# Gathered chunks of a graph layer rounded and split in pairs, in a ring of six gathered rows and six rounded rows

## The reference

```python
Q = jax.nn.relu(x @ Wq + bq)
V = x @ Wv + bv
# _former: Q = relu(layer_norm(Q)); H from the row sums of Q
out = cosQ @ (cosQ.T @ V) + sinQ @ (sinQ.T @ V)      # divided by a norm per row
# _gcn: deg counts the edges of each dst, dinv = rsqrt(deg)
xw = x @ Wg
gcn = segment_sum(xw[src] * (dinv[src] * dinv[dst])[:, None], dst, N) + bg
y = jax.nn.relu(_layer_norm(out + gcn + V, gamma, beta))
x = _layernorm(x + y, axis=-1)
```

## Time and profile before

| | |
|---|---|
| median of 3 runs | 2114.59 us (2107.7 to 2127.57) |
| the profiled execution | 2113.34 us, span from first to last instruction 2111.5 us |
| granted TensorE clock, mean | 0.908 |
| busy: PE, PEld (weight load) | 1769.9 us (84%), 1402.0 us (66%) |
| busy: DVE, ACT, POOL | 1695.7 (80%), 899.8 (43%), 996.5 us (47%) |
| gathers (L396) | 882, 256 KB each |
| casts (L464), subtractions and one-hots (L769, L766) | 882 of each |

### The profile page before, as it was taken

The page is one execution under the profiler, slowest core; times in us unless marked ns, Lnnn a source line. Parts: engine busy times, 40 slices in busy tenths (PEclk is TensorE's granted clock), DMA queues, the critical chain, the costliest instruction groups (busy, mean ns, idle before and its releaser), DMA issues.

```text
span 2111.5 us, 29877 instructions
## 1 busy us (share of the span) xinstructions
PE 1769.9 (84%) x8579; PEld 1402.0 (66%) x8579; DVE 1695.7 (80%) x3686; ACT 899.8 (43%) x1642; POOL 996.5 (47%) x1056
## 2 busy tenths in 40 slices
PE   3888827999979997979997989988988887997986
PEld 2666625777757774857775867766776676775775
DVE  6888866898868887858776778877887997987997
ACT  1222214556545555535554456655333333332332
POOL 0000006666656666567665657677333443443440
PEclk9999968999989997989998889989888898887897
DMA  3111167877757877667776758767554654654662
GB/s 111 61 51 61 51 226 240 257 249 240 252 177 243 258 231 218 190 197 234 222 231 183 212 182 259 232 217 231 170 165 130 204 180 138 192 173 142 192 192 83
DMA packets 159968, 394.66 MB, mean 187 GB/s; under 512 B 23760, under 2 KB 25420, under 8 KB 159796
## 3 DMA queue, kind: packets, MB, share of 16 engines
q0 software_dynamic: 71120, 233.10, 37.6%
q1 hardware_dynamic: 67544, 121.07, 17.0%
q10 hardware_dynamic: 21132, 38.50, 5.1%
HBM read 341.24 MB, written 51.34 MB: 186 GB/s over the span
## 4 chain that ended last, share of the span: by engine, by line
PE 51%; DVE 30%; issue 9%; ACT 5%; DMA 3%; DVEq 1%; POOL 0%; POOLq 0%; another core or an unknown queue 0%; ACTq 0%; SPq 0%
PE bank L1041 10%; PE bank L1042 10%; PE bank L1040 10%; PE bank L1117 9%; PE bank L1119 7%; DVE stage L716 5%; DVE split L769 3%; DVE bn_parts L964 2%; DVE stage L713 2%; DMA split<-scaled_g,index_slots 2%; DVE rows L769 2%; ACT split L464 2%; PE bank L1070 2%; DVE one_hot L766 2%; DVE operands L726 1%
## 5 line engine op out<-in xcount | busy, mean ns | idle before, releaser
L396 POOL DMA_INDIRECT split<-scaled_g,index_slots x490 | 521.1, 1063 | 395.8 <-PE bank L1119 251.4
L396 POOL DMA_INDIRECT rows<-scaled_g,index_slots x392 | 415.3, 1059 | 210.8 <-PE bank L1119 96.8
L464 ACT CAST split<-split 128x512 fp32r<-128x512 f32 x490 | 299.6, 617 | 427.4 <-PE bank L1119 267.4
L1117 PE MATMUL bank<-split,one_hot 128*128 128x512 f32 x882 | 390.4, 443 | 104.4 <-DVE combine L799 38.2
L769 DVE TENSOR_TENSOR split<-split 128x512 fp32r<-128x512 f32 x490 | 339.4, 693 | 66.0 <-ACT split L464 55.2
L464 ACT CAST split<-rows 128x512 fp32r<-128x512 f32 x392 | 240.4, 618 | 284.0 <-PE bank L1119 222.6
L1040 PE MATMUL bank<-weights,operands 128*128 128x512 f32 x784 | 334.4, 427 | 1.4 <-DVE operands L813 1.4
L1041 PE MATMUL bank<-weights,operands 128*128 128x512 f32 x784 | 322.0, 411 | 0.0
L1042 PE MATMUL bank<-weights,operands 128*128 128x512 f32 x784 | 320.0, 408 | 0.0
L766 DVE TENSOR_SCALAR one_hot<-tile_id,dst_cols 128x128 fp32r<-128x128 f32 x882 | 257.5, 292 | 69.0 <-PE bank L1119 47.2
L1117 PEld LDWEIGHTS bank<-split,one_hot 128*128 128x128 f32 x882 | 172.7, 196 | 183.8 <-DVE rows L769 59.0
(11 more groups left out here) (194 smaller groups left out, 2941.9 us busy)
## 6 DMA issues: line engine op xcount, KB each, us to landing
stage<-in_x SPq DMA_DIRECT2D x144, 256.0 KB, 2.8
stage<-values SPq DMA_DIRECT2D x98, 256.0 KB
scaled_g<-nodes SPq DMA_DIRECT2D x49, 256.0 KB, 3.1
own_rows<-scaled_g SPq DMA_DIRECT2D x49, 256.0 KB
values<-stage ACTq DMA_DIRECT2D x49, 256.0 KB
combine<-values SPq DMA_DIRECT2D x49, 256.0 KB
gcn_plus_values<-combine ACTq DMA_DIRECT2D x49, 256.0 KB
stage<-gcn_plus_values SPq DMA_DIRECT2D x49, 256.0 KB
```

The lines of the kernel that those rows point to most:

```text
L396: pool.indirect_dma_start(out=plain(row_ring[k % RING]), out_offset=None, in_=table, in_offset=bass.IndirectOffsetOnAxis(ap=index_slots[:, ...
L464: act.copy(hi_ring[k % SPLIT], plain(row_ring[k % RING])).then_inc(s["chunk_rounded"], 1)
L1117: pe.matmul(gcn_bank[:, :], one_hot[:, slot, :], hi_ring[slot], start=k == 0, stop=False, skip_group_check=True)
```

## The change

Rows and rounded rows are kept in three pairs each. `split[:, 0:6]` holds the rounded rows, `split[:, 6:8]` and the four rows of `rows` the gathered ones. ACT and DVE act at even k only: ACT waits for both landings of the pair and for `chunk_summed` with `freed(n + 1, 6)` (with n even, the sum of chunk n-5), and rounds 1024 columns at once. DVE makes both one-hots behind one wait (six slots of one-hots now) and subtracts 1024 columns at once. `chunk_rounded` and `chunk_split` count pairs. POOL still gathers each row by itself, into six slots. PE's instructions and their order are the same; it waits for the split at even k only. The extra chunk uses slot 0 as before.

```diff
--- before.py
+++ after.py
@@ -44,8 +44,9 @@
     GROUPS = -(-CHUNKS // P)
     HIST = -(-CHUNKS // TILES)
     PER_TILE = 18
-    RING = 9
-    SPLIT = 3
+    RING = 6
+    SPLIT = 6
+    PAIRS = 3
     BATCH = 6
     COLS = GROUPS * P
     LN_EPS = 1e-5
@@ -153,7 +154,9 @@
                 for n in range(3)]
         g_hi, g_lo = split[:, 0:4, :], split[:, 4:8, :]
         hi_ring = [split[:, n, :] for n in range(SPLIT)]
-        row_ring = [split[:, SPLIT + n, :] if n < 5 else rows[:, n - 5, :] for n in range(RING)]
+        hi_pairs = [split[:, 2 * n:2 * n + 2, :] for n in range(PAIRS)]
+        row_pairs = [split[:, 6:8, :], rows[:, 0:2, :], rows[:, 2:4, :]]
+        row_ring = [row_pairs[n // 2][:, n % 2, :] for n in range(RING)]
 
         def plain(ap):
             return ap.bitcast(F32)
@@ -387,7 +390,7 @@
                 for k in range(PER_TILE):
                     if k % BATCH == 0:
 
-                        wait_apart(pool, s["chunk_rounded"], freed(chunk_number(seq, k + BATCH - 1), PER_TILE))
+                        wait_apart(pool, s["chunk_rounded"], freed(chunk_number(seq, k + BATCH - 1) // 2, PER_TILE // 2))
                         pool.tensor_copy(index_slots[:, k:k + BATCH], src_cols[:, bass.ds(first + k, BATCH)])\
                             .then_inc(s["chunk_indexed"], 1)
                         pool.wait_ge(s["chunk_indexed"], done(seq * (PER_TILE // BATCH) + k // BATCH))
@@ -458,10 +461,12 @@
 
 
             def chunk(seq, k):
-                n = chunk_number(seq, k)
-                act.wait_ge(landed[k % RING], seq * (16 * PER_TILE // RING) + 16 * (k // RING + 1))
-                act.wait_ge(s["chunk_summed"], freed(n, SPLIT))
-                act.copy(hi_ring[k % SPLIT], plain(row_ring[k % RING])).then_inc(s["chunk_rounded"], 1)
+                if k % 2 == 0:
+                    n, pair = chunk_number(seq, k), k // 2 % PAIRS
+                    for r in (k % RING, k % RING + 1):
+                        act.wait_ge(landed[r], seq * (16 * PER_TILE // RING) + 16 * (k // RING + 1))
+                    act.wait_ge(s["chunk_summed"], freed(n + 1, SPLIT))
+                    act.copy(hi_pairs[pair], plain(row_pairs[pair])).then_inc(s["chunk_rounded"], 1)
 
             def extra_chunks(seq):
                 first = act.value_load(column(schedule, seq), min_val=0, max_val=CHUNKS - 1)
@@ -760,13 +765,16 @@
                 return first
 
             def chunk(seq, k, first):
-                n = chunk_number(seq, k)
-
-                dve.wait_ge(s["chunk_summed"], freed(n, SPLIT))
-                dve.tensor_scalar(one_hot[:, k % SPLIT, :], tile_id[:, :], column(dst_cols, first + k), None,
-                                  ALU.is_equal).then_inc(s["chunk_hot"], 1)
-                dve.wait_ge(s["chunk_rounded"], done(n))
-                dve.tensor_tensor(row_ring[k % RING], plain(row_ring[k % RING]), plain(hi_ring[k % SPLIT]), ALU.subtract)\
+                if k % 2:
+                    return
+                n, pair = chunk_number(seq, k), k // 2 % PAIRS
+
+                dve.wait_ge(s["chunk_summed"], freed(n + 1, SPLIT))
+                for c in (k, k + 1):
+                    dve.tensor_scalar(one_hot[:, c % SPLIT, :], tile_id[:, :], column(dst_cols, first + c), None,
+                                      ALU.is_equal).then_inc(s["chunk_hot"], 1)
+                dve.wait_ge(s["chunk_rounded"], done(n // 2))
+                dve.tensor_tensor(row_pairs[pair], plain(row_pairs[pair]), plain(hi_pairs[pair]), ALU.subtract)\
                     .then_inc(s["chunk_split"], 1)
 
             def add_own(seq):
@@ -1113,7 +1121,8 @@
                 if k == 0:
 
                     pe.wait_ge(s["gcn_combined"], freed(seq, 1))
-                pe.wait_ge(s["chunk_split"], done(chunk_number(seq, k)))
+                if k % 2 == 0:
+                    pe.wait_ge(s["chunk_split"], done(chunk_number(seq, k) // 2))
                 pe.matmul(gcn_bank[:, :], one_hot[:, slot, :], hi_ring[slot], start=k == 0, stop=False,
                           skip_group_check=True)
                 pe.matmul(gcn_bank[:, :], one_hot[:, slot, :], row_ring[k % RING], start=False, stop=False,
```

## The result

The changed kernel takes 2271.59 us (median of four runs, 2258.16 to 2276.42), beside 2115.98 us for the kernel before in the same comparison: a ratio of 1.072, 95% interval 1.065 to 1.079. It is slower by 7.2%, where 2174 us was forecast, and the time lies 17 us above the range (2105 to 2255). The profiled execution has a span of 2267.2 us, 155.7 more than before.

A forecast was written before the change was run, and what follows sets the result against it. PE was taken to bound the Q/V, cosine and sine stages, DVE and PE both full in the output stage. Pauses +60, output stage -6 and refills +7 made +61 on 2113 us: 2174 us, range 2105 to 2255.

The forecast's parts named there:

- a loop of 7.2 us: From the sum that frees a slot to the pair's first matmul on PE: 7.2 us, between 6.35 and 8.1.
- a landing of 4.1 us: Gather start to cast start: 4.1 us, the middle of 3.24 (drained kernel) and 4.96 (full flow).
- two or three equal pauses a tile: PE pauses once per ring turn: 2 a tile in Q/V and sine, 3 in cosine; 60 us in all.
- the refills: After each of seven extra chunks the rings refill with longer cast and subtraction: +1.0 us each, +7 us.
- a rival at 0.10: Pauses also lower PE's clock to 0.85 in Q/V, cosine and sine: 108 us more, 2282 us; chance 0.10.
- the 0.6 us a tile of the forecast: Merging DVE instructions saves 0.07 us a pair, 9 pairs a tile, where DVE is never idle: 0.6 us.
- 4.96 at all places: Slow end of gather start to cast start: pauses of 142 us, of which 7/8, and 2257 us in all.
- 0.75 us: Time from a freed row slot to the start of the next gather on POOL: 0.75 us.
- 0.48 each: PE's pause in each ring turn of the cosine stage: 0.48 us, 3 a tile, 12 tiles, 17 us.
- the 0.90 that was forecast: PE's pause in a ring turn of the Q/V stage: 0.90 us, 2 a tile, 16 tiles, 29 us.
- What is queued behind the waiting instructions makes this no smaller: Next tile's rounding on ACT and splitting on DVE, held behind cast and subtraction, do not reduce the 60 us.
- -6: Output stage: merge gain less stalls, plus waits removed, -0.5 us a tile for 12 tiles: -6 us.

The follow-up runs named there:

- e2: Kernel before with gathered rows cut from 9 to 6 slots and rounded rows raised from 3 to 6, rows handled singly: 2148.28 us, ratio 1.015.
- e1: Kernel before with only its ring of gathered rows cut from 9 to 6 slots, rows handled singly: 2173.06 us, ratio 1.026.
- e3: Changed kernel, still in pairs, with 8 gathered and 4 rounded slots in place of 6 and 6: 2129.6 us, ratio 1.017.
- e6: Changed kernel, still in pairs, with 10 gathered and 4 rounded slots in place of 6 and 6: 2106.02 us, ratio 1.009.
- e9: Kernel before, rows handled singly, with 8 gathered and 4 rounded slots in place of 9 and 3: 2089.65 us, ratio 0.983.
- e4: Changed kernel with DVE's combine moved ahead of the first pair's subtraction, behind its one-hots: 2241.54 us, ratio 1.060.
- e12: Changed kernel, in pairs, with 10 gathered and 4 rounded slots and the combine ahead of the first pair's subtraction: 2120.12 us, ratio 0.998.
- e13: Kernel before, single rows, with 10 gathered and 4 rounded slots and the combine behind chunk 0 in place of chunk 1: 2090.65 us, ratio 0.984.
- e15: Kernel before, single rows, with 8 gathered and 4 rounded slots and the combine behind chunk 0 in place of chunk 1: 2048.8 us, ratio 0.980.

## Why the prediction was wrong in size

Two steps of the sum failed. The pauses of PE were mis-sized: a loop of 7.2 us with a landing of 4.1 us at every place, and two or three equal pauses a tile, gave 60 us, 67 with the refills, and PE's time outside its busy time grew by 110. And the busy time of PE was taken as unchanged, its clock left to a rival at 0.10; it grew by 44.

**Right: direction, mechanism and place.** PE pauses in the three stages that it bounded; casts wait for landings; PE's idle time is released by DVE, by the pair's subtraction (86.0 + 21.8 us) and more still by the combine that stands behind it (114.2); POOL waits for PE's sums (259.4 + 233.5 us); no gain and no loss in the output stage. The short ring and the pair together are the cause: the short ring alone costs 1.5 to 2.6% (e2, e1), pairs with eight and ten rows 1.7 and 0.9% (e3, e6), both together 7%.

**Right: the durations.** Subtraction 1223 ns and cast 1047 ns, forecast 1.22 and 1.05 us. The Trainium skill (VectorE: DVE Perf Modes, Side-by-side: where the cycles go) gives the fixed part as about 150 cycles, and these durations fit it. The changed kernel did not get that time back: its output tiles are 50.6 us as before, and 49.0 with the same slots handled singly (e2). With eight rows they are 49.7 in pairs and 49.0 singly (e3, e9). In these paired kernels the combine stands behind the first pair. With the combine moved they are 48.4 and 48.8 in pairs (e4, e12) and 49.3 and 48.9 singly (e13, e15), so that the 0.6 us a tile of the forecast may be there once the combine is out of its way; no two kernels differ in this alone.

**Wrong: the landing, 4.1 us as one value for all places.** From the trace of the changed kernel, the medians from the start of a pair's second gather to its landing (over tiles that neither hold nor follow an extra chunk) lie between 3.3 and 5.6 us by the chunk's place in the tile. At the places that hold PE up they are the long ones: 4.9 at chunk 12 of Q/V, 5.2 at chunk 2 of cosine, 5.6 at chunk 2 of sine, single ones 6.3 as in the timeline above. The middle of two ends was taken, but the pause goes by the slowest place in each turn of the ring. The trace of the kernel before already had this spread: its medians by place run from 3.4 to 4.9 us in the three stages. The prediction had its own answer to this: with 4.96 at all places it gave 142 us for the pauses, of which 7/8, and 2257 in all. The Trainium skill (DMA: Bandwidth & Descriptors, Anatomy of one DMA), which gave an estimate of 2.6 us, is off here by more than the prediction was.

**Wrong: from the slot to the gather, 0.75 us.** That is the least. At the start of a tile POOL reads the schedule and makes indices first: medians of 1.7 us at chunk 2 of cosine. With the landing, the loop that ends at chunk 2 took 10.4 us in cosine (median), 9.9 in sine. At that place in sine the queues add to it as well: 1.0 us from landing to cast and 0.8 from cast to subtraction (medians), where the sum had 0.03 for the second, and the first inside its 4.1.

**Wrong: the count and the place of the pauses.** "where the tile's end stands in one turn (...), I count 2", for Q/V and sine, took the start of a tile for a place where a pause is hidden behind a wait that PE has anyway, and in cosine three equal pauses were counted. In cosine and sine the start of the tile is where the pauses are largest. From one chunk's start on PE to the next (medians, before to after): chunk 2 of cosine 1.49 to 3.10 us, chunk 2 of sine 1.16 to 3.38. Of the 4.1 us by which the medians of a cosine tile grew in sum, 3.5 are ahead of its chunk 6; the later turns, for which 0.48 each was forecast, hardly pause. In Q/V there are three: 0.54 at chunk 0, 0.95 at chunk 6, which is the 0.90 that was forecast, and 2.02 at chunk 12.

**Wrong: "What is queued behind the waiting instructions makes this no smaller", counted at nothing more.** It made it larger. `x_split` behind the late pair holds PE's products (22.4 us in all), and the combine behind the first pair adds to PE's waits; e4 bounds what the combine's place alone is worth to about 1 point, some 25 us, in the output stage.

**Wrong: the clock, a rival at 0.10.** "Pauses of about 1 us are short" was the reason against it. The granted clock fell from 0.97, 0.90 and 0.94 to 0.95, 0.88 and 0.93. By the trace's clock records a tile of Q/V, cosine and sine spends 1.4, 1.7 and 1.6 us more at the lower level than before; at half speed that loses half of it, for 16, 12 and 8 tiles 28 us. So the rival's mechanism came in beside the forecast's, at a quarter of the rival's full price. The rest of the 43.9 us more of busy time was not traced further.

The account then is: pauses 110 us where 60 + 7 was forecast; busy PE 44 where 0 was; output stage about 0 where -6 was. The two causes were weighed as alternatives, and they came together: with more and longer pauses came more time at the lower clock.

**What stays open:** why landings are slower at some places, the start of a cosine or sine tile and chunk 12 of Q/V. Other transfers of 256 KB and gathers issued in short order may be the reason, but no run changed either. Open is also how much of the pauses is the landing and how much is queued work, since every experiment changed the room in the rings or the order on DVE, and none the landing.

## What to carry to other kernels

To shorten a ring, add up its loop (slot free, issue, landing, each engine's pass, what is queued ahead on each) at every place of the period and take the slowest, not a mean; the start of a period, where other work is queued, is likely to be it. Merging two items into one instruction adds the second item's landing and both items' longer passes to that loop, and puts other work on these engines behind two items. Here it gave nothing back with six or eight rows, and some tenths of a microsecond a tile at most where the engine that it relieves was full and the combine was moved. Before giving slots from one ring to another, try the rings' sizes with the code as it is: the same twelve slots as 8 and 4 in place of 9 and 3 were worth 1.7%. And compare kernels from different sets of runs only where they differ by more than the kernel before itself moves between the sets.

## What the hardware did that was not expected

- A gather of 256 KB took from 3.3 us (median at the quiet places) to over 6 us from its start on POOL to its landing, in one kernel, by place in the tile, with the DMA engines at a mean share of only 0.63 to 0.68.
- PE standing for about 2.8 of 4.2 us was followed by 5.7 us at a granted clock of 0.50, in the middle of a stage at 0.95; of 47 pauses over 1.4 us, 21 had such a fall in them or shortly behind.
- A merge of 441 pairs of DVE instructions took 52.7 us off DVE's recorded busy time (1695.7 to 1643.0) and 18.7 of it in the output stage (529.75 to 511.07), where DVE is fullest; that stage did not get shorter.
